# GpSimd adds only key tiles 0 and 1 of the probabilities; TensorE takes tiles 2 and 3 straight into the denominators

## What is computed

```
x = x + attention(layernorm(x), ctx, ctx)      # 32 query heads, 8 key/value heads, head width 32
x = x + ffn(layernorm(x), ...)                 # gated choice among 8 small experts
# attention: softmax(q k^T / sqrt(32)) v, over 512 queries and 512 keys for each head
```

## Time and profile before

| | us |
|---|---|
| median of 3 runs | 1024.77 |
| lowest, highest | 1020.37, 1025.66 |
| span of the profiled execution, first to last instruction | 1023.9 |
| PE busy | 949.4 (93%) |
| DVE busy | 904.8 (88%) |
| POOL busy | 794.4 (78%) |
| ACT busy | 761.3 (74%) |

### The profile page before, as it was taken

How to read it: one execution, slowest core, us unless ns; L and a number is a source line. 1 busy time by engine, 2 the same in 40 slices (tenths; PEclk the granted TensorE clock), 3 DMA queues, 4 the chain that set the end, 5 groups by cost and what they waited for, 6 DMA issues and landing times.

```text
span 1023.9 us, 24706 instructions
## 1 busy us (share of the span) xinstructions
PE 949.4 (93%) x9518; PEld 372.5 (36%) x9518; DVE 904.8 (88%) x1138; ACT 761.3 (74%) x1333; POOL 794.4 (78%) x422
## 2 busy tenths in 40 slices
PE   4789999999999999999999999999999999999996
PEld 3223233333333232333333333332222226777773
DVE  6869999999999999999999999998888876888976
ACT  7468888888888888888888888888777777554440
POOL 7158999999999999999999999998999998222110
PEclk9989999999999999999999999999999999999998
DMA  7675677767677767676767686766555744766423
GB/s 247 184 167 114 161 154 168 156 162 159 155 158 167 168 152 170 145 171 150 180 143 175 138 188 134 182 122 154 119 119 139 165 95 141 247 213 236 148 104 164
DMA packets 319876, 164.19 MB, mean 160 GB/s; under 512 B 182216, under 2 KB 307240, under 8 KB 319760
## 3 DMA queue, kind: packets, MB, share of 16 engines
q1 hardware_dynamic: 319456, 161.76, 64.3%
q0 software_dynamic: 304, 0.85, 0.3%
HBM read 107.58 MB, written 54.53 MB: 158 GB/s over the span
## 4 chain that ended last, share of the span: by engine, by line
PE 36%; DVE 30%; issue 25%; ACT 5%; POOL 2%; DMA 1%; SPq 0%; DVEq 0%; POOLq 0%; ACTq 0%
DVE row_max L949 14%; PE psum L589 8%; PE psum L603 6%; PE psum L616 5%; PE psum L734 5%; DVE den_t L961 4%; PE psum L551 4%; ACT probs L884 3%; PE psum L712 3%; DVE o_t L955 3%; PE psum L577 2%; DVE probs L1161 2%; DVE prod_mem L1008 2%; PE psum L700 1%; ACT prod_mem L824 1%
## 5 line engine op out<-in xcount | busy, mean ns | idle before, releaser
L884 ACT ACTIVATE probs<-psum 128x512 f32<-128x512 f32 x1024 | 554.7, 596 | 106.7 <-PE psum L589 88.7
L949 DVE TENSOR_REDUCE row_max<-psum 128x4 f32<-128x2048 f32 x248 | 566.0, 2282 | 63.5 <-PE psum L551 63.1
L589 PE MATMUL psum<-q_stack,k_stack 97*32 97x512 f16 x4096 | 335.0, 386 | 10.2 <-issue 3.6
L363 POOL TENSOR_TENSOR sums<-probs 128x2048 f32<-128x2048 f32 x63 | 287.8, 4568 | 19.5 <-ACT probs L884 19.5
L351 POOL TENSOR_TENSOR sums<-probs 128x2048 f32<-128x2048 f32 x63 | 287.2, 4558 | 10.2 <-PE psum L626 5.5
L603 PE MATMUL psum<-probs,v_in 128*32 128x512 f32 x2048 | 268.9, 598 | 1.0
L589 PEld LDWEIGHTS psum<-q_stack,k_stack 97*32 97x32 f16 x4096 | 96.8, 95 | 258.7 <-ACT probs L884 148.6
L551 PE MATMUL psum<-high_mem 32*128 32x512 f16 x992 | 98.3, 385 | 23.7 <-DVE row_max L949 20.0
L323 POOL TENSOR_TENSOR o_t<-o_t,inv 128x512 f32<-128x512 f32 x64 | 67.1, 1048 | 44.2 <-DVE inv L967 44.2
L328 POOL TENSOR_TENSOR o_all<-o_all,o_t 128x512 f32<-128x512 f32 x64 | 81.5, 1274 | 9.5 <-POOL o_t L323 0.4
L603 PEld LDWEIGHTS psum<-probs,v_in 128*32 128x32 f32 x2048 | 59.4, 111 | 61.1 <-issue 16.7
(11 more groups left out here) (120 smaller groups left out, 788.9 us busy)
## 6 DMA issues: line engine op xcount, KB each, us to landing
q_stack<-q_split SPq DMA_DIRECT2D x192, 128.0 KB, 3.4
xa<-in_x_dram SPq DMA_DIRECT2D x32, 512.0 KB, 4.7
o_all<-in_x_dram SPq DMA_DIRECT2D x256, 64.0 KB, 2.5
x_attended<-o_all SPq DMA_DIRECT2D x64, 256.0 KB, 4.1
out_dram<-probs SPq DMA_DIRECT2D x32, 512.0 KB, 2.9
q_split<-prod_mem SPq DMA_DIRECT2D x15, 1024.0 KB, 5.4
xa<-x_attended SPq DMA_DIRECT2D x16, 512.0 KB, 4.5
probs<-x_attended SPq DMA_DIRECT2D x16, 512.0 KB, 5.3
```

The costliest lines, as they stand in the source:

```text
L363: pool.tensor_tensor(sums[:, 2 * u % SUMS], probs[:, u % 2, 0], probs[:, u % 2, 1], ALU.add).then_inc(front_done, 1)
L589: last = pe.matmul(st_ps[row:row + D, bank_of["score", u, n], :], k_stack[:, u % SLOTS, t * P + row:t * P + row + D], q_stack[:, u % SLOTS ...
L884: act.activation(probs[:, s, keys, g, :], st_ps[:, bank_of["score", u, n], :], ACT.Exp, scale=EXP_SCALE).then_inc(exped, 1)
L949: dve.reduce_max(row_max[:, u % 2, t:G * ST:ST], s_ps[:], AX.X).then_inc(reduced, 1)
```

## The change

GpSimd's back sum and its semaphore go. `last_denominators` of units 0 to 62 multiplies ones with key tile 2 and with key tile 3 of `probs`, four matmuls each, instead of four matmuls on the sum. Everything that waited for `back_done` now waits for `den_done`. Unit 63 is as before.

```diff
@@ gpsimd, main loop
-                    if 0 <= u - 1 < UNITS - 1:
-                        wait(pool, exped, NSC * u)
-                        wait(pool, den_done, u - 1)
-                        pool.tensor_tensor(sums[:, (2 * u - 1) % SUMS], probs[:, (u - 1) % 2, 2],
-                                           probs[:, (u - 1) % 2, 3], ALU.add).then_inc(back_done, 1)
@@ sync, before the loads of the second part
-                        sp.wait_ge(back_done, u + 1)
+                        sp.wait_ge(den_done, u + 1)
@@ tensor, last_denominators(u)
                     if u == UNITS - 1:
                         pe.wait_ge(last_sums, 2)
+                        left = (sums[:, (2 * u + 1) % SUMS],)
                     else:
-                        pe.wait_ge(back_done, u + 1)
-                    for g in range(G):
-                        last = pe.matmul(st_ps[g * D:(g + 1) * D, bank_of["den", u, 0], :], ones[:, 0:D],
-                                         sums[:, (2 * u + 1) % SUMS, g, :], start=False, stop=True)
+                        pe.wait_ge(exped, NSC * (u + 1))
+                        left = (probs[:, u % 2, 2], probs[:, u % 2, 3])
+                    for term in left:
+                        for g in range(G):
+                            last = pe.matmul(st_ps[g * D:(g + 1) * D, bank_of["den", u, 0], :], ones[:, 0:D],
+                                             term[:, g, :], start=False, stop=term is left[-1])
                     last.then_inc(den_done, 1)
@@ scalar, before an exponential of unit u
-                                    wait(act, front_done if keys < ST // 2 else back_done, u - 1)
+                                    wait(act, front_done if keys < ST // 2 else den_done, u - 1)
@@ scalar and vector, second part, first use of the memory of probs
-                            act.wait_ge(back_done, UNITS - 1)
+                            act.wait_ge(den_done, UNITS - 1)
-                        dve.wait_ge(back_done, UNITS - 1)
+                        dve.wait_ge(den_done, UNITS - 1)
```

More of the change, by code:

```diff
@@ L165, in xattn_ffn @@
             shift_made, scored, exped, pv_done = sem("shift_made"), sem("scored"), sem("exped"), sem("pv_done")
-            front_done, back_done, den_done = sem("front_done"), sem("back_done"), sem("den_done")
+            front_done, den_done = sem("front_done"), sem("den_done")
             last_sums = sem("last_sums")
```

## The result

The changed kernel takes 1073.19 us (median; 1070.22 to 1073.30), beside 1023.07 us for the kernel before in the same comparison. The ratio is 1.0484, with a 95% interval from 1.045 to 1.0519. Forecast were 1071.5 us and a range from 1051 to 1082.

What follows compares the result with a forecast made beforehand. The prediction took the hand-over between TensorE's `score_rows` and VectorE's reduction as the bound. 44.4 us for 30 pairs, 1.7 for unit 62 and 0.55 at the junction made 46.7, hence 1071.5 us, range 1051 to 1082.

Steps and rivals of the forecast that it cites:

- A group takes 0.86 us: Each added group of four matmuls in `last_denominators` of units 0 to 62 takes 0.86 us from TensorE's stream.
- rival 2: Additions cost more than their spacing: 1.07 us a group, all 63 uncovered, 67 us in all, 1092 us; chance 0.05.
- Quarter 0 costs 0.62: Even unit, behind `score_rows`: TensorE's lead absorbs part of the 0.86 us, so the next reduction starts 0.62 us later.
- Quarter 3 costs 0.86: End of the even unit: VectorE has no slack, so `score_rows` to `score_rows` grows by the whole 0.86 us.
- Quarters 1 and 2 carry the shift: Even unit, no additions there: the 0.62 us from quarter 0 are passed on and nothing is won back.
- No wait by `den_done`: Both places in even units: `den_done` comes before VectorE reaches `take_denominators`, so this step adds no wait.
- GpSimd gives nothing in the loop: Removing 63 back sums, 287.2 us of GpSimd, gains nothing in the loop, as they ran beside other work.
- 0.87 us around the span: Whole launch: 0.87 us outside the profiled span, added to a span of 1070.6 to give 1071.5 us.
- The junction: Passage to the second part: only 0.31 us of the freed GpSimd's gain usable, den 62 adds 0.86; net +0.55 us.
- Rival 1: Only one of the two places costs, quarter 0 being absorbed: 27.5 us more, 1052 us; chance 0.07.
- rival 3: GpSimd sets the beat: extra groups fall into gaps, the junction comes forward by up to 3.99 us, 1020.8; chance 0.05.
- rival 4: Nothing moves: additions hidden, the junction bound by TensorE, 1024.8 us; chance 0.03.

Runs made afterwards that it cites:

- the three sizes: Quarter 0 of even units: extra group of 128 or 256 columns in the kernel before, 512 by direct even denominators in the changed kernel: ratios 1.0001, 1.0084, 1.0217.
- the runs at single places: Changed kernel with only even units' denominators direct (quarter 0): 1045.22 us, ratio 1.0217; with only odd units' direct (quarter 3): 1050.70 us, ratio 1.0274.

## Why the prediction was right, point by point

**The profiled execution, split by five points of the timeline.** Starts of L626 (L624 after) and of L700 (L698 after):

| stretch | before | after | difference | forecast |
|---|---|---|---|---|
| start to `last_denominators` in unit 2 | 77.79 | 75.85 | -1.94 | 0 |
| 30 pairs, to the same place in unit 62 | 753.72 | 799.42 | +45.70 | +44.4 |
| to the first L700 | 23.34 | 25.91 | +2.57 | +2.58 |
| to the L700 of the second batch entry | 12.21 | 11.89 | -0.32 | -0.31 |
| to the end | 156.84 | 155.23 | -1.61 | 0 |
| sum | 1023.90 | 1068.30 | +44.40 | +46.7 |

(The group of unit 62 starts at 831.51 before and at 875.27 after.) The middle three stretches give 47.95 us. The two outer ones, in which the change adds nothing, hide 3.55 us of it in this pair of profiles. In the medians of the comparison the difference is 50.1 us. The forecast started from 1024.77, and 1073.19 is 48.4 above that.

Of the 1.61 us in the last stretch 1.37 lie in one group, the last results, which takes 10.20 us before and 8.83 after, and there the granted clock differs. Windows of it, before and then after:

```profile
1010.00:1015.00 5.00, 5.00 (x8) 1.90 (x7) 2.25 (x6) 0.00 (x0) 0.00 (x0) 0.50 0.48 198
```

```profile
1055.00:1060.00 5.00, 5.00 (x9) 2.00 (x8) 3.07 (x8) 0.00 (x0) 0.00 (x0) 0.66 0.51 210
```

Before, TensorE ran these 5 us at half its full clock, that is at 1.2 GHz of 2.4; after, for part of them only. In the 5 us ahead of these windows it had been busy for 1.84 us only, in both kernels, as it waited for the last gates. Of the 1.94 us in the first stretch only about half goes with the clock. TensorE stands still near 60 us, for 3.64 us before and 2.69 after, while ScalarE waits for the transfer of `k_split` (3.43 and 2.40 us); that is 0.95 us. Behind it the clock is low (0.66 of full clock from 60 to 70 us before, 0.83 after), and the way to L626 takes 14.23 us before and 13.34 after; that is 0.89 us. Why one execution gets the longer wait and less of the clock no run here shows.

**Step by step.**
- *A group takes 0.86 us.* Right: 0.85 us more to the successor of L624 in quarter 0, 0.86 in quarter 3. The Trainium skill's 131 ns for a matmul ("TensorE: Matmul & The Clock Gate", "Back-to-back issue gap") would make it 1.05 us, by an estimate. L624 takes 1.74 us for 16 records, 109 ns each. So rival 2, with 1.07 us a group, is out; what spoke for it, that ScalarE writes `probs` beside the group, does not occur.
- *Quarter 0 costs 0.62.* 0.63 measured, with the free part shown by the three sizes.
- *Quarter 3 costs 0.86.* 0.85 measured.
- *Quarters 1 and 2 carry the shift.* Right but for 0.03 to 0.04 us in quarter 1. The reduction at 509.68 takes 2.29 us, where the earlier trace rows shows 2.25 for the one that follows the transpose without a gap. Times 30 that is the larger part of the 1.3 us by which the pairs were forecast too low.
- *No wait by `den_done`.* Right: `take_denominators` at 507.83 and 518.19 follows its reduction at once. In `take_rows` a wait of 0.25 us came up, as forecast, inside the same gap. That the reduction would idle "some 0.6 us" was put wrongly: 0.43 of it are seen as idle, split over these two; the rest is overlap between neighbouring instructions of DVE that was lost.
- *GpSimd gives nothing in the loop.* Shown by keeping its back sum.
- *0.87 us around the span.* This compared a median with the span of another execution. The profiled execution of the changed kernel took 1070.22 us with a span of 1068.3, so that 1.9 us lie around it. The forecast doesn't suffer, as it is also the median and 46.7.
- *The junction.* The numbers came out (+2.57, -0.32), the reason only half. I took the 0.31 us for the gain from the freed GpSimd. With the back sum kept, the same distance is 11.90 us. TensorE's later arrival alone closes the gap, as it gives GpSimd's chain time to be done: ScalarE's step ahead of that L700 begins 10.92 us after the first L700 before, 8.97 with the sum kept and 6.87 after. The last 2.1 us are what the removal gives, and nothing uses them. So the 0.31 us came out right by luck. The margin is thin: with 128 columns more in quarter 3 alone, and the back sum kept, the distance is 11.90 as well, with the step at 10.59.
- *The rivals.* Rival 1 (one place free) and rival 3 (GpSimd sets the beat) ended with the runs at single places and with the sum kept, rival 4 (nothing moves) with the result.

No run here with the whole denominators beats the kernel before. The run without the second groups shows how little there is to gain on this side: with TensorE 1.77 us a pair lighter the loop is 0.04 us shorter. That relief on TensorE would pay together with relief on VectorE is what this suggests; no run tried it.

## What to carry to other kernels

In a loop where two engines hand over to one another several times, price an edit by the place where it stands, not by the share of busy time: read from the timeline which engine arrives last at that hand-over, and by how much. That room (here some 0.22 us in one quarter, almost none in another) is free, and beyond it every further bit costs its full time. A balanced loop is lopsided: 1.71 us of TensorE's work more cost 1.52 us a pair and 1.77 us less gave back 0.04, while 287 us taken from a third engine that was 78% busy gave nothing.

## What the runs showed of the hardware

- Float32 matmuls in four column groups side by side, 128 rows by 32 columns of weights, take from the stream 0.24 us for eight records of 128 columns, 0.45 for 256 and 0.86 to 0.89 for 512. The time goes with the columns down to 128; the weight loads of about 0.11 us each did not show as a floor.
- A group that reads `probs` and one that reads `sums` take the same: 26.84 us a pair both ways. ScalarE writes no part of `probs` during the direct groups. The `gather`, which reads `probs` while ScalarE writes another part of it (507.67 and 507.76 after), takes 0.87 us from the stream, where a group on `sums` takes 0.88 to 0.89.
